# Projecting the context's keys and values for the last attention during an earlier expert stage

## The reference

```python
def layernorm(x, g, b):
    mu = jnp.mean(x, axis=-1, keepdims=True)
    var = jnp.var(x, axis=-1, keepdims=True)
    return (x - mu) * jax.lax.rsqrt(var + EPS) * g + b
# xn: layernorm of the context; ln: layernorm of the (already normalised) x
# keys and values come from concatenate([xn, ln]) @ Wkv : 512 keys per row, 8 heads of 64
# queries come from ln @ Wq; softmax over the 512 keys; then @ Wo and a layernorm, added to x
```

## Time and profile before

| what | us |
|---|---|
| median of 3 runs | 3864.73 (3860.83 to 3868.84) |
| the profiled execution | 3874.34 |
| its span, first to last instruction | 3872.6 |
| PE busy in the span | 3004.4 (78%) |
| DVE busy | 2374.5 (61%) |
| ACT busy | 1782.8 (46%) |
| DMA, mean over the span | 64 GB/s |
| mean granted clock of TensorE | 0.893 |

### The profile page before, as it was taken

One profiled execution on the slowest core, in us unless ns is written; L12 is line 12 of the kernel. 1 busy time (PEld: TensorE's weight loads), 2 busy tenths in 40 slices (PEclk: granted clock), 3 DMA queues, 4 the chain that ended last, 5 costly groups with the idle time before them and its releaser, 6 DMA issues. The chain is left out here.

```text
span 3872.6 us, 55118 instructions
## 1 busy us (share of the span) xinstructions
PE 3004.4 (78%) x18581; PEld 2159.9 (56%) x18581; DVE 2374.5 (61%) x5302; ACT 1782.8 (46%) x4243; POOL 696.8 (18%) x817
## 2 busy tenths in 40 slices
PE   4899988998877698477777554695696669898697
PEld 3667766676656476354555323344694445555485
DVE  5776777667666334777777676997114855555323
ACT  4666666666431222577677262403232235555121
POOL 0000000000110412255345000000210013323422
PEclk7999999999988799799899777797798879999799
DMA  3111111011100476000000000001692000000476
GB/s 100 44 34 39 45 36 34 28 47 31 44 1 1 160 251 228 16 2 2 26 9 1 25 0 2 2 0 45 248 341 71 1 26 2 2 1 1 159 232 214
DMA packets 96630, 246.93 MB, mean 64 GB/s; under 512 B 15936, under 2 KB 62272, under 8 KB 91360
## 3 DMA queue, kind: packets, MB, share of 16 engines
q1 hardware_dynamic: 87520, 219.56, 16.9%
q0 software_dynamic: 8688, 23.78, 1.6%
q10 hardware_dynamic: 144, 0.07, 0.0%
HBM read 204.21 MB, written 39.15 MB: 63 GB/s over the span
## 5 line engine op out<-in xcount | busy, mean ns | idle before, releaser
L2876 POOL TENSOR_TENSOR L0a_sum_sq<-L0a_sum_sq,L0a_sq 128x512 f32<-128x512 f32 x56 | 76.8, 1371 | 967.6 <-ACT L0a_sq L2818 967.6
L1190 POOL TENSOR_TENSOR L3x_p<-L3x_p,L3x_rsum 128x512 f32<-128x512 f32 x128 | 132.9, 1039 | 506.7 <-DVE L3x_rsum L1270 506.7
L2922 DVE SCALAR_TENSOR_TENSOR L0a_xf<-L0a_xc,L0a_conv,L0a_xf 128x256 f32<-128x256 f32 x432 | 191.3, 510 | 30.9 <-ACT L0a_xf L2783 29.6
L2734 ACT ACTIVATE L0a_ex<-bank,L0a_nb 128x128 f32<-128x128 f32 x512 | 144.6, 369 | 97.1 <-PE bank L2665 96.5
L1251 DVE SCALAR_TENSOR_TENSOR L3x_s<-bank,L3x_bias 128x512 f32<-128x512 f32 x128 | 86.5, 681 | 155.0 <-PE bank L1034 154.8
L2931 DVE TENSOR_TENSOR L0a_ru<-bank,L0a_um 128x512 f32<-128x512 f32 x128 | 88.0, 687 | 151.3 <-PE bank L2657 146.3
L2585 PE MATMUL bank<-x_feat,L0a_wx 128*128 128x256 f32 x576 | 151.8, 413 | 18.8 <-DMA L0a_wx<-in_L0a_wx 13.1
L1885 PE MATMUL bank<-L2a_half,L2a_diag 128*128 128x512 f32 x328 | 144.1, 601 | 27.9 <-ACT L2a_diag L1868 27.9
L1190 POOL TENSOR_TENSOR L1x_p<-L1x_p,L1x_rsum 128x512 f32<-128x512 f32 x128 | 132.2, 1040 | 135.6 <-DVE L1x_rsum L1270 135.6
L1194 POOL TENSOR_TENSOR L1a_p<-L1a_p,L1a_rsum 128x128 f32<-128x128 f32 (+1 forms) x256 | 123.0, 506 | 135.3 <-DVE L1a_rsum L1270 133.3
L2585 PEld LDWEIGHTS bank<-x_feat,L0a_wx 128*128 128x128 f32 x576 | 113.3, 205 | 46.9 <-DMA L0a_wx<-in_L0a_wx 13.3
(11 more groups left out here) (731 smaller groups left out, 8298.3 us busy)
## 6 DMA issues: line engine op xcount, KB each, us to landing
L2f_wt<-in_L2f_w SPq DMA_DIRECT2D x23, 2180.0 KB
L0f_wt<-in_L0f_w SPq DMA_DIRECT2D x39, 898.0 KB
L3f_wt<-in_L3f_w SPq DMA_DIRECT2D x39, 768.0 KB
L0a_wx<-in_L0a_wx SPq DMA_DIRECT2D x72, 256.0 KB, 3.1
L0a_wz<-in_L0a_wz SPq DMA_DIRECT2D x32, 512.0 KB, 4.4
L0f_xs<-rows_by_expert SPq DMA_DIRECT2D x39, 128.5 KB
L3f_xs<-rows_by_expert SPq DMA_DIRECT2D x39, 128.5 KB, 3.2
rows_by_expert<-L0f_zeros SPq DMA_DIRECT2D x4, 1028.0 KB
```

Source lines behind the costliest of these rows:

```text
L1190: last = nc.gpsimd.tensor_tensor(both, both, rsum[r % 2][:, i, :].unsqueeze(2).to_broadcast([P, S, NK]), ALU.mult)
L2734: last = a(ex[g % 3][:, j, b * P:(b + 1) * P], bank[:, at:at + P], ACT.Exp, bias=nb[r % 2][:, b, h:h + 1])
L2922: vec.scalar_tensor_tensor(out=xf[q % 4][:, j, :], in0=xc[q % 3][:, j, i:i + T], scalar=conv[:, 2 * p + j, i:i + 1], in1=xf[q % 4][:, j, : ...
```

## The change

In `routed` for `L2f`, VectorE now also takes the statistics of `c.ctx` and normalises it in place, ahead of its wait for the logits. PE turns it (`turn_context`), one block of 512 tokens before the wait for `taken` and three after the counting. ACT copies it to `c.ctxT` with the last attention's gain and shift, the first block ahead of the exponential. SP loads the affine vectors and the k and v weights. Then 32 items, each 2 matmuls of 512 columns into one bank (`project_context`), give the context's keys and values. ACT copies each bank to one of four staging buffers and issues a DMA of 256 KB to device memory (`store_context`). 14 items stand before the first slot and 18 after the last `fall`. ACT waits at the end until the stores have landed.

In the last attention the block that loads `affine`, the context's norm and `c.ctxn` are gone, and the second norm of `x` takes the place of the context's norm, in the block that loads the weights. For this attention the context's k and v units and the copies `cb` are gone. SP fetches both halves for each row with two DMAs of 512 KB, into `kT` and `v` directly. The remaining units stand at other steps: q at 0 and 1, k at 2 and 5, v at 4 and 6, and none at 3 and 7. The other attentions keep their order. Cut to its core, the diff is (the `OWN` offsets in the unit indices are left out):

```diff
...
+        self.kv_rows = nc.dram_tensor("context_keys_values", [B, P, 2 * KD * BLK], F32).ap()
...
+        if context:
...
+            ctx_w, ctx_ln = sb("ctx_w", [P, 2, KD, BLK]), sb("ctx_ln", [P, 4, KD])
+            c_stats, c_mv, c_rstd = sb("c_stats", [P, NT, 6]), sb("c_mv", [P, NT, 2]), sb("c_rstd", [P, NT, 3])
+            staged = [zeros[:, i * BLK:(i + 1) * BLK] for i in range(4)]
+        IN_FRONT, CTX_ITEMS = (14, 8 * NBLK) if context else (0, 0)
+        T_FIRST = KD * NBLK * (2 if context else 1)
...
+                if context:
+                    sp.dma_start(ctx_ln[:], w[f"{context}_ln"]).then_inc(sig("ctx_w"), 16)
+                    sp.dma_start(ctx_w[:, 0], w[f"{context}_wk"]).then_inc(sig("ctx_w"), 16)
+                    sp.dma_start(ctx_w[:, 1], w[f"{context}_wv"]).then_inc(sig("ctx_w"), 16)
...
+                def turn_context(n):
+                    pe.wait_ge(sig("c_normed"), n + 1)
+                    for k in range(KD):
+                        bank = t_ring.claim(pe)
+                        for j in range(4):
+                            last = nc.tensor.transpose(bank[:, j * P:(j + 1) * P], c.ctx[:, 4 * n + j, k * P:(k + 1) * P], c.ident[:])
+                        t_ring.fill(last)
...
+                def project_context(i):
+                    n, q = divmod(i, 8)
+                    if i == 0:
+                        pe.wait_ge(sig("ctx_w"), 16 * 3)
+                        pe.wait_ge(t_ring.emptied, T_FIRST)
+                    bank = r_ring.claim(pe)
+                    for k in range(KD):
+                        if q < 4:
+                            last = mm(bank[:], ctx_w[:, 0, k, q * P:(q + 1) * P], c.ctxT[:, k, n * BLK:(n + 1) * BLK],
+                                      start=(k == 0), stop=(k == KD - 1))
+                        else:
+                            t = 4 * n + q - 4
+                            last = mm(bank[:], c.ctxT[:, k, t * P:(t + 1) * P], ctx_w[:, 1, k, :], start=(k == 0), stop=(k == KD - 1))
+                    r_ring.fill(last)
...
+                if context:
+                    turn_context(0)
                 pe.wait_ge(sig("taken"), 1)
...
                     fall_shared(len(EARLY) - 1)
+                if context:
+                    for n in range(1, NBLK):
+                        turn_context(n)
+                for i in range(IN_FRONT):
+                    project_context(i)
                 turn(0)
...
                 fall(S - 1)
+                for i in range(IN_FRONT, CTX_ITEMS):
+                    project_context(i)
...
+                def take_context(n):
+                    for k in range(KD):
+                        bank = t_ring.take(act)
+                        t_ring.empty(a(c.ctxT[:, k, n * BLK:(n + 1) * BLK], bank[:], ACT.Identity,
+                                       bias=ctx_ln[:, 3, k:k + 1], scale=ctx_ln[:, 2, k:k + 1]))
...
+                def store_context(i):
...
+                    n, q = divmod(i, 8)
+                    if i >= 4:
+                        act.wait_ge(sig(f"kv_out{i % 4}"), 16 * (i // 4))
+                    bank = r_ring.take(act)
+                    r_ring.empty(a(staged[i % 4], bank[:], ACT.Copy))
+                    act.wait_ge(r_ring.emptied, r_ring.n_out)
+                    if q < 4:
+                        to = c.kv_rows[2 * n:2 * n + 2, :, q * T:(q + 1) * T].rearrange("r p t -> p r t")
+                        act.dma_start(to, staged[i % 4].rearrange("p (r t) -> p r t", r=2)).then_inc(sig(f"kv_out{i % 4}"), 16)
+                    else:
+                        r, j = divmod(4 * n + q - 4, TB)
+                        to = c.kv_rows[r, :, 4 * T + j * BLK:4 * T + (j + 1) * BLK]
+                        act.dma_start(to, staged[i % 4]).then_inc(sig(f"kv_out{i % 4}"), 16)
...
+                if context:
+                    act.wait_ge(sig("c_var"), 1)
+                    a(c_rstd[:, :, 1], c_rstd[:, :, 0], ACT.Sqrt).then_inc(sig("c_std"), 1)
+                    act.wait_ge(sig("ctx_w"), 16 * 3)
+                    take_context(0)
                 act.wait_ge(sig("centred"), 1)
                 a(prob[:], prob[:], ACT.Exp).then_inc(sig("exp"), 1)
+                if context:
+                    for n in range(1, NBLK):
+                        take_context(n)
+                    act.wait_ge(sig("cleared"), 16 * ((S + 7) // 8))
+                    for i in range(IN_FRONT):
+                        store_context(i)
                 for q in range(len(EARLY)):
...
+                for i in range(IN_FRONT, CTX_ITEMS):
+                    store_context(i)
+                if context:
+                    for i in range(4):
+                        act.wait_ge(sig(f"kv_out{i}"), 16 * CTX_ITEMS // 4)
...
+                if context:
+                    for t in range(NT):
+                        last = v.bn_stats(c_stats[:, t, :], c.ctx[:, t, :])
+                    ch.link(last)
+                    for t in range(NT):
+                        last = v.bn_aggr(c_mv[:, t, :], c_stats[:, t, :])
+                    ch.link(last)
+                    v.tensor_scalar_add(c_rstd[:, :, 0], c_mv[:, :, 1], 1e-5).then_inc(sig("c_var"), 1)
+                    dve.wait_ge(sig("c_std"), 1)
+                    ch.link(v.reciprocal(c_rstd[:, :, 2], c_rstd[:, :, 1]))
+                    for n in range(NBLK):
+                        for t in range(4 * n, 4 * n + 4):
+                            last = v.tensor_scalar(c.ctx[:, t, :], c.ctx[:, t, :], c_mv[:, t, 0:1], c_rstd[:, t, 2:3], ALU.subtract, ALU.mult)
+                        last.then_inc(sig("c_normed"), 1)
                 dve.wait_ge(sig("logits"), 1)
                 if biases:
                     ch.link(v.tensor_tensor(prob[:], logits, each(gate_b), ALU.add))
...
-                        dve.wait_ge(r_ring.filled, 2 * (s - 2))
+                        dve.wait_ge(r_ring.filled, 2 * (s - 2) + IN_FRONT)
...
-    routed(c, "L2f", 1, 1024, gated=False, biases=True)
+    routed(c, "L2f", 1, 1024, gated=False, biases=True, context="L3x")
...
+    OWN = 1 if kind == "latent" else 0
...
-        UNITS = [[("k", 0)], [("k", 1)], [("q", 0)], [("q", 1)], [("v", 0)], [("k", 2), ("v", 1)], [("k", 3), ("v", 2)], [("v", 3)]]
+        UNITS = [[("q", 0)], [("q", 1)], [("k", 0)], [], [("v", 0)], [("k", 1)], [("v", 1)], []]
...
-                K_UNITS = MQ * (NK // T) // 2
+                K_UNITS = MQ * (NK // T - OWN) // 2
...
                             sp.dma_start(mask[r % 2][:, 0, :], w["mask_bool"][row_of(r)].to_broadcast([P, T])).then_inc(sig(f"mask{r % 2}"), 16)
+                            if r >= 2:
+                                sp.wait_ge(sig("weighted"), (r - 1) * PER_ROW)
+                            sp.dma_start(kT[r % 2][:, :, 0:T], c.kv_rows[r, :, 0:MQ * T].rearrange("p (m t) -> p m t", m=MQ)).then_inc(sig(f"kv{r % 2}"), 16)
+                            sp.dma_start(v[r % 2][:, 0:TB, :], c.kv_rows[r, :, MQ * T:].rearrange("p (j d) -> p j d", j=TB)).then_inc(sig(f"kv{r % 2}"), 16)
...
+                                if kind == "latent":
+                                    pe.wait_ge(sig(f"kv{r % 2}"), 32 * (r // 2 + 1))
                             scores(u + 1)
...
-                                last = nc.scalar.activation(own(v[r % 2][:, i, e * C:(e + 1) * C]), own(bank[:, 0:C]), ACT.Copy)
+                                last = nc.scalar.activation(own(v[r % 2][:, i + OWN * TB, e * C:(e + 1) * C]), own(bank[:, 0:C]), ACT.Copy)
...
                     def slice_c(r):
-                        src = c.ctxn if kind == "latent" else c.ctxT
-                        vec.tensor_copy(cb[r % 2][:], src[:, :, bass.ts(row_of(r), T)]).then_inc(sig("sliced_c"), 1)
+                        if kind == "latent":
+                            return
+                        vec.tensor_copy(cb[r % 2][:], c.ctxT[:, :, bass.ts(row_of(r), T)]).then_inc(sig("sliced_c"), 1)
...
-        c.ctxn = sb("ctxn", [P, KD, N])
-        affine = sb("affine", [P, 4, KD])
-        c.load("L3xn_ld", [(affine[:], c.dram["L3x_ln"])])
-        with ExitStack() as inner:
-            xn = c.tiles(inner, "L3xm")("xn", [P, NT, D])
-            normalise(c, "n3x", c.x, dst=xn)
-
-            normalise(c, "n3y", xn, dstT=c.xT, gain=affine[:, 0, :], shift=affine[:, 1, :])
+        xn, affine = sb("xn", [P, NT, D]), sb("affine", [P, 4, KD])
+        normalise(c, "n3x", c.x, dst=xn, loads=[(affine[:], c.dram["L3x_ln"])])
         softmax_attention(c, "L3x", 8, 64, 4, 4, 64, "latent", 1.0 / 64.0,
-                          norm=dict(src=c.ctx, dstT=c.ctxn, gain=affine[:, 2, :], shift=affine[:, 3, :]))
+                          norm=dict(src=xn, dstT=c.xT, gain=affine[:, 0, :], shift=affine[:, 1, :]))
```

22 lines of the change are left out of this document (12 added, 10 removed).

## The result

| kernel | median, us | runs |
|---|---|---|
| before | 3862.78 | 3864.73, 3860.83, 3868.84, 3856.48 |
| after | 3820.93 | 3805.71, 3819.32, 3822.54, 3822.55 |

The ratio is 0.9884 (95% interval 0.9863 to 0.9905), or 42 us less, where 49.8 us less were forecast. The profiled execution of the changed kernel took 3805.71 us (span 3803.9), so the two profiles lie 68.7 us apart. About 18 us of that isn't the change's, as the last experiment shows.

A forecast was written before the change was run, and what follows sets the result against it. PE was taken to bound the last attention, with idle stretches in the expert stage as cover. +25.8 - 19.6 - 8.5 - 47.5 = -49.8 us gave 3824.5 from the profiled 3874.3, or 3815 us from the median; range 3803 to 3827.

The forecast's parts named there:

- Routing: Third layer's expert stage: VectorE's context normalise costs nothing; the exponential and all routing behind it come 3.1 us later.
- The 2.4 us for a slow start: Before the expert slots: the 14 items start at the half clock, which costs 2.4 us.
- It fits with nothing to spare: Before the slots: weights and scatter (6.9 MB) plus stores (3.7 MB) at 352 GB/s need 30 us, about what there is.
- rival (b): Item stores are slow: a 10 us landing with four staging buffers gives 2.5 us an item, 24 us more, 3839 us; chance 0.04.
- Behind the slots: After the last `fall`: 18 items take 31.3 us, then copy, issue and landing; the expert stage ends 25.8 us later overall.
- Norms: Blocks before the last attention: the load block (2.3 us) and one normalise of two (17.3 us) go, -19.6 us.
- The lead-in of row 0: Last attention before its first scores: half of the four k and four v units goes, -8.5 us.
- Rows: Last attention's steady part: 7 rows each lose 7.28 us of PE work less 0.5 us of stalls, -47.5 us.
- (a): Attention rows shrink less, held by VectorE and ACT at steps 4 to 6: 17.5 us more, 3833 us; chance 0.17.
- (d): PE's clock falls in the attention's emptier steps: up to 45 us, time about 3860, no change; chance 0.05.
- The 0 that I took for the outputs: Attention's output matmuls, 3.69 or 5.38 us by the clock: change may bring -5 to +7 us, taken as 0.
- Rival (c): Stores land after 18.0 us, so an item takes 4.5 us: 88 us more, 3903 us; chance 0.06.

The follow-up runs named there:

- the last experiment: The changed kernel run again, unchanged, against the kernel before: 3824.96 against 3874.71 us, ratio 0.9878; untouched expert stages differed by 3.6 to 12.9 us between executions.

## Why the prediction was right, and where it wasn't

The predicted 3815 us stand against 3820.93, and the sum of -49.8 us against -42 (-53 to -37 by the interval) in the first comparison, -49.8 in the second, and -50.6 in the stages. That it fits so well is luck in part. Two errors in front worked against each other and left 4.1 us more than my sum, and the other terms together brought 4.9 us more than I had said: 0.9 behind the slots, 0.8 in the norms, 1.4 ahead of row 0 and 1.8 in the rows.

- **Routing.** VectorE's new chain costs nothing, as said. The exponential starts 2.8 us later against the stage's start, where 3.1 were said, and the experiment that puts it first gives 3.3 us back.
- **Front, first error.** The items start at +42.2 us (said: 43.0), at the full clock and not at half: the granted clock was 0.57 from 2728.0 to 2730.3 and 1.00 from there on, so it had risen during the 24 transposes ahead of the items. The 2.4 us for a slow start weren't paid. With the stores cut, `rise(1)` starts at +71.1, where my sum had +74.8.
- **Front, second error.** "It fits with nothing to spare" is the step that failed. I had set 10.6 MB at 352 GB/s against 30 us, the rate extrapolated from the share of 0.73. With the stores added the engines are full (share 1.00, 1.03 and 1.08 in three of the four stretches), but move 408, 319 and 346 GB/s there, and 296 in the mean of the 40 us. Seven eighths of the stores' bytes cost 78.9 - 71.1 = 7.8 us, where I had put their cost at nothing. Together with the first error `rise(1)` came 10.7 us later than before, where I had 6.6.
- **The landing.** I took 3.1 us for a store. It is 3.5 without the weights. Beside them it is 10.2 in the median and 14.9 to 16.3 for the first four. So rival (b), an item held by four tiles and a landing of 10 us, was true in front and only there. Its price was not the one I gave it: more tiles moved the wait and gained nothing. Behind the slots, where queues are empty, ACT waited 2.5 us in all.
- **Behind the slots.** From the last `fall` to the next stage it was 20.2 us and became 38.5, +18.3, where my sum had +19.2. The 18 items took 1.72 us each, and VectorE was long done, as said.
- **Norms.** -20.4 us against -19.6. The lead-in of row 0 was -9.9 against -8.5.
- **Rows.** 48.0 us a row against 54.85 - 6.78 = 48.07. Both are rows with an output of 5.38 us, and (a), which would have shown in rows over 50 us, fell. The clock of the whole stretch stayed at 0.97, and in the bare steps at 1.00, so (d) fell. It falls in one place of a row, at the output: 0.68 there, after a wait of 1.89 us, and 1.00 in the steps with gaps of 0.4 to 0.6 us. The Trainium skill's TensorE: Matmul & The Clock Gate, "A second HAM failure mode: psum-queue depth-cycling", which the prediction quoted, tells of a clock that swings where PE pauses often between groups; the trace does not show that for the gaps between steps. The 0 that I took for the outputs held, by luck: four of eight took 5.38 us before and after, but six of eight in four other profiles of this attention. That is 3.4 us. The q units ahead of row 0 took 3.72 to 6.49 us, and the attention 388.2 to 394.5 over all these profiles.
- **Rival (c)** decided from a landing of 13 us. In front the median came within 3 us of that and the first four stores were past it, but the tail never came near it (6.8 us at most).

## What to carry to other kernels

An idle engine is cover for that engine's work and for nothing else: work moved there brings its bytes, and a DMA share of 0.73 was already too full for them. When a wait on a buffer ends a stall, look at the DMA share before adding buffers. Here, at a share of 1, more depth moved the wait to whoever was next in the queues, and fewer bytes in that stretch, or another stretch, were what helped. Items of independent work can be dealt out over several small idle places, as many in each as its covering chain is long. Here a third place took about 14 us off (280.0 less 3.3 for the exponential and 1.4 for the order, against 261.6). Read a median landing with care as well: it can mix stores that stand beside a large load with stores that don't.
